# Two small row transfers of an attention kernel, issued by SP in place of ACT

## The reference

```python
xn = layernorm(x)
q, k, v = split(xn @ qkv_w.T + qkv_b, 3)            # 16 heads of 16 columns
scores = einsum("bqhd,bkhd->bhqk", q, k) / sqrt(16)
scores = where(causal, scores + slopes * (k_pos - q_pos), -1e9)
attn = softmax(scores) @ v
s = attn @ out_w.T + out_b
g = silu(moe(xn))                                    # top 2 of 8 experts
x = x + s * g
```

## Time and profile before

| | |
|---|---|
| median of 3 runs | 816.44 us (815.64 to 819.16) |
| the profiled execution | 815.3 us, its span 813.5 us |
| busy in the span | PE 83%, DVE 74%, ACT 58%, POOL 34% |
| mean granted PE clock | 0.938 |
| DMA | 85.84 MB, mean 106 GB/s; q1 71114 packets, q10 2386 |
| transfers of line 811 | 64, of 3 KB each |

### The profile page before, as it was taken

The page is one execution under the profiler, slowest core; times in us unless marked ns, Lnnn a source line. Parts: engine busy times, 40 slices in busy tenths (PEclk is TensorE's granted clock), DMA queues, the critical chain, the costliest instruction groups (busy, mean ns, idle before and its releaser), DMA issues.

```text
span 813.5 us, 14740 instructions
## 1 busy us (share of the span) xinstructions
PE 678.5 (83%) x5306; PEld 312.0 (38%) x5306; DVE 601.9 (74%) x1222; ACT 475.5 (58%) x990; POOL 279.3 (34%) x458
## 2 busy tenths in 40 slices
PE   3478859769889888989898898889898989898885
PEld 1234545433233433444344444443443443232432
DVE  5999776689777786787678777867886788688342
ACT  2276685860566575666565665666565656666551
POOL 2313442027723323333323433233333234660112
PEclk9889889985899999999999999999999999799998
DMA  9710324634450453244233323522442221350001
GB/s 293 251 65 0 97 73 160 200 130 149 161 145 1 124 152 87 71 124 125 72 86 127 93 74 111 148 83 79 134 127 72 80 90 46 88 185 14 27 32 47
DMA packets 76852, 85.84 MB, mean 106 GB/s; under 512 B 34169, under 2 KB 60284, under 8 KB 76412
## 3 DMA queue, kind: packets, MB, share of 16 engines
q1 hardware_dynamic: 71114, 74.05, 30.0%
q0 software_dynamic: 3280, 8.98, 3.5%
q10 hardware_dynamic: 2386, 1.87, 0.8%
HBM read 39.54 MB, written 27.53 MB: 82 GB/s over the span
## 4 chain that ended last, share of the span: by engine, by line
PE 55%; ACT 18%; DVE 13%; issue 7%; ACTq 3%; DMA 2%; SPq 1%; POOL 1%; POOLq 0%; DVEq 0%
PE bank L1575 16%; ACT PR L830 11%; PE bank L1511 9%; PE bank L1469 8%; DVE PM L1233 5%; PE bank L1534 5%; PE bank L1483 4%; PE bank L1341 3%; ACTq L811 3%; PE bank L1589 2%; PE bank L1384 2%; PE bank L1614 2%; ACT TG L788 1%; ACT U L819 1%; DMA qk_parts<-TG 1%
## 5 line engine op out<-in xcount | busy, mean ns | idle before, releaser
L830 ACT ACTIVATE PR<-bank 128x512 f32<-128x512 f32 (+3 forms) x640 | 317.1, 537 | 226.0 <-PE bank L1534 127.4
L1233 DVE TENSOR_REDUCE PM<-bank 128x1 f32<-128x512 f32 (+3 forms) x640 | 354.3, 604 | 73.6 <-PE bank L1511 46.4
L1534 PE MATMUL bank<-OPS 57*128 57x512 f16 (+3 forms) x640 | 209.6, 363 | 53.4 <-ACT PR L830 48.3
L1511 PE MATMUL bank<-OPS 54*128 54x512 f16 (+3 forms) x640 | 195.8, 372 | 10.5 <-DVE PM L1233 7.0
L1575 PE MATMUL bank<-PR,VS 128*17 128x512 f32 (+3 forms) x1280 | 161.2, 556 | 0.0
L1511 PEld LDWEIGHTS bank<-OPS 54*128 54x128 f16 x640 | 50.2, 95 | 129.6 <-DVE PM L1233 86.9
L1534 PEld LDWEIGHTS bank<-OPS 57*128 57x128 f16 x640 | 54.0, 94 | 117.6 <-ACT PR L830 109.1
L1469 PE MATMUL bank<-WB 128*128 128x256 f16 x552 | 81.2, 277 | 0.0
L600 POOL CAST POSB<-YT 128x256 f16<-128x256 f32 x46 | 18.2, 396 | 173.8 <-DVE YT L1135 173.8
L1469 PEld LDWEIGHTS bank<-WB 128*128 128x128 f16 x552 | 48.2, 98 | 32.5 <-issue 25.9
L1544 PE MATMUL bank<-MASK 64*128 64x64 bf16 x512 | 59.5, 199 | 0.0
(11 more groups left out here) (185 smaller groups left out, 893.2 us busy)
## 6 DMA issues: line engine op xcount, KB each, us to landing
WB<-W SPq DMA_DIRECT2D x23, 512.0 KB, 3.6
OPS<-qk_parts SPq DMA_DIRECT2D x60, 192.0 KB
x_rows<-PR SPq DMA_DIRECT2D x23, 256.0 KB, 3.3
WB<-in_w SPq DMA_DIRECT2D x23, 256.0 KB, 3.5
y_rows<-XT SPq DMA_DIRECT2D x23, 256.0 KB, 3.0
W<-in_w SPq DMA_DIRECT2D x6, 512.0 KB, 5.7
XT<-in_b SPq DMA_DIRECT2D x23, 128.0 KB, 3.9
XO<-in_x SPq DMA_DIRECT2D x4, 512.0 KB, 13.0
```

What stands on the lines that cost most here:

```text
L830: act.activation(PR[:, tile % RING, off:CH], PS[2 + tile % 2][:, off:CH], ACT.Exp, scale=1 / SCORE).then_inc(b_exped, 1)
L1233: dve.tensor_reduce(PM[:, c % 2, j, xq, gg:gg + 1], bank[:, 0:width], AX.X, ALU.max).then_inc(a_reduced, 1)
L1511: last = mm(bank[:, 0:width], OPS[ROWS_A, slot, 0, P * (TC * a + xq):P * (TC * a + xq) + P], OPS[ROWS_A, slot, 1, CH * gg:CH * gg + width] ...
L1534: last = mm(bank[:, off:CH], OPS[ROWS_B, slot, 1, P * k:P * k + P], OPS[ROWS_B, slot, 0, CH * b + off:CH * b + CH], start=True, stop=k < T ...
```

## The change

`rows_out` is written on SP in place of ACT, with the same wait and the same two transfers, and SP calls it first in the same step of its own loop, ahead of the fetch, the store and the loads of that step. ACT keeps `max_rows`. Nothing else is changed.

```diff
@@ SP
+            def rows_out(m):
+
+                p, a = m // NC, ORDER[m % NC]
+                sp.wait_ge(mt_copied, m + 1)
+                for j in range(2):
+                    sp.dma_start(OPS[ROWS_MAX, (2 * p + j) % 4, 0, CH * a:CH * a + CH].rearrange(
+                        "j (q t) -> j q t", q=TC), MT[3 * TC * j:3 * TC * j + 3 * TC, m % 2, :]).then_inc(mrow[m % NC], 16)
+
...
             for n in range(STEPS):
+                if n - 2 in TURN_AT:
+                    rows_out(TURN_AT[n - 2])
                 if n in FETCH_AT:
                     fetch_block(FETCH_AT[n])
@@ ACT
-            def rows_out(m):
-
-                p, a = m // NC, ORDER[m % NC]
-                act.wait_ge(mt_copied, m + 1)
-                for j in range(2):
-                    act.dma_start(OPS[ROWS_MAX, (2 * p + j) % 4, 0, CH * a:CH * a + CH].rearrange(
-                        "j (q t) -> j q t", q=TC), MT[3 * TC * j:3 * TC * j + 3 * TC, m % 2, :]).then_inc(mrow[m % NC], 16)
...
-                if n - 2 in TURN_AT:
-                    rows_out(TURN_AT[n - 2])
```

## The result

The changed kernel takes 884.6 us (median of 4 runs, 882.2 to 888.2) against 816.45 us: a ratio of 1.083, 95% interval [1.079, 1.087]. The forecast was 885.5 us, in a range of 855 to 912. The profiled execution of after is the longest of its four runs (888.2 us, span 886.4); its span is 72.9 us longer than that of before.

What follows compares the result with a forecast made beforehand. No engine is full; ACT's 64 row issues hold up exponentials that in-order PE awaits. 815.3 - 11.8 (ACT) + 44.7 (pairs) + 27.2 (start) + 9.0 (clock) = 884.4, as a median 885.5 us, range 855 to 912.

Steps and rivals of the forecast that it cites:

- What bounds the kernel, and program order: ACT's issues delay exponentials; on SP, rows come late behind loads at the start, other places except chunk 2's harmless.
- The seven places: PE stalls at the first b score of all and at chunk 2's first b score in pairs 1 to 6.
- The queue: On q1 rows wait behind load packets on the same three DMA engines: +44.7 us in pairs, +27.2 at the start.
- The reading by which only the time on the sequencer changes: The skill's rule: transfers share 16 engines and interleave, so the sum would be only ACT's gain, -11.8 us.
- the first rival: Rows wait on q1 only as on q10: +13.6 at the start, +14 in pairs 1 to 5, 832 us; chance 0.11.
- the right end of the bound: Rows' wait on q1 taken as its upper end, the following store's landing: 11.2 us in pair 1, 15.2 in pair 6.
- The gain on ACT: Behind chunks 3, 0 and 1, PE's waits for exponentials go: 1.47 us in each of 8 pairs, -11.8 us.
- The clock: After five stalls of about 8 us PE's clock falls to 0.50, 1.8 us each: +9.0 us (0 to 18).
- the small gap of pair 6: Ahead of chunk 2 in pair 6, a PE stall of 2.9 us, not among the five charged for the clock.
- The end: The reload of x1 behind the last rows lands about 758.0, before POOL's reader: cost 0, at most 1 us.
- The sum: For the whole kernel, 815.3 - 11.8 + 44.7 + 27.2 + 9.0 = 884.4, as a median 885.5 us.

Runs made afterwards that it cites:

- x9_only_one: The kernel before with only the rows of chunk 2 of pair 0 issued by SP, the other 62 transfers by ACT: 830.4 us, ratio 1.011.
- x6_spread: The changed kernel in its order, each head's loads cut into transfers of 16 rows (outer dimension 16 in place of 3): 831.9 us, ratio 1.016.
- x5_late_on_act: The kernel before, all rows on ACT, but chunk 2's rows of pairs 1 to 6 issued ten steps later: 855.3 us, ratio 1.041.
- x7_spread_behind: The changed kernel, all rows on SP, with the loads moved behind the rows and cut to outer dimension 16: 803.0 us, ratio 0.980.
- x2_chunk2_act: The changed kernel, but chunk 2's rows of pairs 1 to 6 issued by ACT again: 825.5 us, ratio 1.009.
- x8_three_act: The changed kernel, but ACT issues rows of chunks 0, 1 and 2 of pair 0 and chunk 2 of pairs 1 to 6: 806.3 us, ratio 0.985.
- x10_before_spread: The kernel before, all rows by ACT, with the loads cut into transfers of 16 rows: 820.8 us against 821.1, ratio 1.0005.

## Why the prediction was right, step by step

**What bounds the kernel, and program order.** Right. The seven places were those named, pair 7 has none, and the rest of SP's list (fetches, stores, chunk 0, 1 and 3's rows) cost no gap. One place was passed over: chunk 2 of pair 0. It has no load in its own pair, and its rows are issued 8 steps before they are needed, but load(2) and load(3) are still draining when it comes. In the changed kernel the longer stall at the start hides it; x9_only_one shows that it costs 9 us uncovered.

**The queue.** The decisive step, and x9_only_one shows it with SP free: the same two transfers that cost nothing on ACT's queue cost 9 us on SP's. The reading by which only the time on the sequencer changes, and the first rival's 13.6 and 14 us, are excluded. That the loads and the rows stand on the same three engines fits x6_spread, where in the pairs the rows land sooner though they are issued hardly earlier. Which engines they are is in no row of these traces.

Taking the landing of the store as the price was the right end of the bound: in the changed kernel the store behind the rows of pair 1, issued at 319.07, lands at 328.5, and PE has had its rows at 328.2. The DMA view of after, 318 to 328 us:

```profile
y_rows<-XT SPq DMA_DIRECT2D x1, 256.0 KB, 9.4
```

Forecast 44.7 us for the pairs, measured 40.4 as gaps and 44.0 as stretches. Forecast 27.2 at the start, measured 25.8 as a gap; the stretch is 27.9, but without the 2.9 us by which the stage began later it is 25.0, 2 us less than forecast.

**The gain on ACT.** Right in its places, and nearly in its size. To see it, stretches at the same granted clock must be compared, for in some pairs the clock falls for a while between chunk 3 and the next chunk 0, whichever engine issues the rows. One such stretch, from pair 1 to pair 2, in windows (as above): before and x5_late_on_act, where ACT issues the rows of chunks 0 and 1, then after and x7_spread_behind, where SP does:

```profile
315.11:347.95 32.84, 29.38 (x246) 12.94 (x245) 22.75 (x44) 18.69 (x41) 10.48 (x17) 0.95 0.33 91
321.55:353.21 31.66, 28.17 (x246) 12.73 (x245) 22.64 (x44) 18.66 (x41) 10.45 (x17) 1.00 0.34 95
...
350.74:381.52 30.78, 27.61 (x247) 12.77 (x245) 22.74 (x45) 18.56 (x41) 11.06 (x18) 1.00 0.35 98
309.99:341.96 31.97, 28.82 (x247) 13.02 (x245) 22.85 (x45) 18.58 (x41) 11.07 (x18) 0.95 0.33 96
```

The relief is 0.9 us, at either clock, and a fall of the clock costs 1.2 us, with either engine. From chunk 2 to chunk 3, at a clock of 1.00 and without a gap, before and x2_chunk2_act:

```profile
294.24:315.11 20.87, 18.92 (x183) 8.44 (x181) 16.63 (x37) 13.76 (x30) 8.78 (x20) 1.00 0.33 100
...
315.69:335.88 20.19, 19.03 (x183) 8.49 (x181) 16.33 (x37) 13.56 (x30) 8.19 (x19) 1.00 0.33 105
```

That is another 0.7 us, behind chunk 3's issue. From chunk 1 to chunk 2 most pairs take 16.34 us in both kernels: chunk 2's issue brings nothing, as forecast. Together 1.6 us in a pair, where 1.47 was forecast; with the first and the last pairs an estimate of some 13 us for the whole stage, against 11.8. In x8_three_act the kernel is 7 to 18 us faster. The 17.7 us of the table hold more than the relief: the clock fell in five of the first six stretches between chunk 3 and chunk 0 in this execution of before, and in one of after. The change is not what spares it: it fell in none of x5_late_on_act (rows on ACT) and in four of x7_spread_behind (rows on SP). Why it falls there is open.

**The clock.** Forecast +9.0, and the stretches behind the gaps are 9.1 us longer. The agreement hides two errors: without a gap these stretches would have been 0.3 to 0.7 us shorter each (x2_chunk2_act), so the price is some 13 us. And the small gap of pair 6, 2.48 us, was put at nothing, yet its stretch is 1.9 us longer; x5_late_on_act says the same of gaps of 1.6 to 4.1 us.

**The end.** The reload of x1 lands 7.7 us after its issue and POOL's first addition waits for it, by 1.2 us (VectorE was through at 821.53), where 0 to 1 was forecast:

```profile
822.73 1.26 POOL L644 TENSOR_TENSOR OPS<-OPS,TG 128x512 f32<-128x512 f32 x1 [11.57 <-DMA OPS<-x_rows]
```

The tail is 9.6 us longer all the same, and that was in no step. Most of it is not the change's. The same windows, 6 us right behind the same 1.59 us gap of PE, first of before, then of x10_before_spread, where the rows and the reload are issued as before:

```profile
762.00:768.00 6.00, 5.82 (x31) 2.61 (x35) 2.39 (x5) 2.71 (x6) 1.09 (x1) 1.00 0.01 3
```

```profile
761.10:767.10 6.00, 5.99 (x17) 2.46 (x18) 0.48 (x1) 1.04 (x2) 0.00 (x0) 0.50 0.01 3
```

The granted clock stayed up in one execution and fell in the other, and the tail of x10_before_spread is 7.1 us longer than that of before. The profiled execution of before, 815.3 us, is at the lower end of that kernel's runs. Why the clock holds in one and not in the other is open, and so is the share of the tail beyond these 7 us.

**The sum.** The two large terms, 71.9 us of the sum, come to 69.0 by the stretches (25.0 for 27.2 and 44.0 for 44.7), the gain to some 13 for 11.8, the clock to 12.8 for 9.0, and the end to 1.2 for nothing: 70 us, where 69.1 was forecast. The mechanism was right, but for the one place passed over. That the time is off by only 0.9 us is partly luck all the same: a start put 2 us too high and a clock put 4 us too low cancel in part, and one execution of a kernel differs from the next by more than that (before ran from 815.3 to 825.9 us in one session).

## What to carry to other kernels

A small transfer that an engine waits for belongs on a queue on which nothing large stands ahead of it; that the issuing engine is idle says nothing of its queue. Look in the trace of before for another transfer at the same place of the same queue: its time to landing is an estimate of the price (it was within 2 us here). Before moving an issue to a free engine, move the bulk loads behind it and spread them over all DMA engines; then the relief of the busy engine is a gain (2% here).

## What the runs showed of the hardware

- A load of 48 rows of 4 KB with an outer dimension of 3 holds 18.8% of the 16 DMA engines; cut to an outer dimension of 16 the queue held 99.5% (x6_spread). The rate went from 77 to 158 GB/s, twice and not five times as much.
- An issue behind many loads takes longer: in before an issue of line 394 takes 0.71 us at the median, and up to 3.0 us within load(2) and load(3); the longest issue of a row transfer on SP took 2.3 us (after).
- Two transfers of 3 KB waited 14 us behind loads on their own queue (x9_only_one), 3.6 to 6.0 us beside them on the other (six places of x5_late_on_act).
- After PE had stood idle from 295.5 to 298.2 us its clock was at 0.50 (1.2 GHz) for the next 6.7 us (x5_late_on_act); after 1.59 us of idle time it was at 0.50 in one execution (x10_before_spread) and at 1.00 in another (before).
